# Storing half of x and loading six experts' down weights in the convolution's time instead of in routing's

## The reference

```python
x = x + attention(layernorm(x))                       # 16 heads, ALiBi
x = x + xattn(ctx, ctx, layernorm(x), ssm_kernel, D)  # long convolution
x = x + ffn(layernorm(x))                             # 8 experts, top 2

# ffn
probs = softmax(hs @ router_gate.T)
topk_scores, topk_idx = top_k(probs, 2)               # scores are then divided by their sum
inter = x_e @ expert_gate_up[e];  gate, up = inter[..., 0::2], inter[..., 1::2]
out_rows = (up * silu(gate)) @ expert_down[e]
out.at[token_slots].add(out_rows * scores)
```

## Time and profile before

| | |
|---|---|
| runs | 1652.3, 1651.71, 1643.85 us; median 1651.71 us |
| profiled execution | 1653.92 us, its span 1652.2 us |
| PE busy | 1477.3 us, 89% of the span |
| DVE, ACT, POOL busy | 1046.5, 764.9, 664.3 us |
| DMA | 172.22 MB, mean 104 GB/s |

### The profile page before, as it was taken

One profiled execution on the slowest core, in us unless ns is written; L12 is line 12 of the kernel. 1 busy time (PEld: TensorE's weight loads), 2 busy tenths in 40 slices (PEclk: granted clock), 3 DMA queues, 4 the chain that ended last, 5 costly groups with the idle time before them and its releaser, 6 DMA issues. The chain is left out here.

```text
span 1652.2 us, 33234 instructions
## 1 busy us (share of the span) xinstructions
PE 1477.3 (89%) x8665; PEld 1192.3 (72%) x8666; DVE 1046.5 (63%) x3146; ACT 764.9 (46%) x2010; POOL 664.3 (40%) x842
## 2 busy tenths in 40 slices
PE   5899999999999999869998799978643999999997
PEld 5788888888888888747776677757642666666665
DVE  4777777777777777756888888886653323333332
ACT  3777777777767677733322323202321332222232
POOL 2011111111111111036886388843665555555553
PEclk9999999999999999979999999985555999999999
DMA  5544434343444343634124011115993555555552
GB/s 160 128 110 107 102 80 102 87 101 90 102 102 102 89 101 90 213 127 145 52 55 155 13 52 57 52 32 179 243 228 80 98 99 99 95 97 98 101 101 44
DMA packets 89776, 172.22 MB, mean 104 GB/s; under 512 B 26384, under 2 KB 26384, under 8 KB 88656
## 3 DMA queue, kind: packets, MB, share of 16 engines
q1 hardware_dynamic: 63584, 122.46, 27.8%
q0 software_dynamic: 18176, 35.80, 12.1%
q10 hardware_dynamic: 7920, 12.93, 3.2%
HBM read 78.10 MB, written 44.79 MB: 74 GB/s over the span
## 5 line engine op out<-in xcount | busy, mean ns | idle before, releaser
L1135 PE MATMUL ps_y<-pairs,taps 128*128 128x288 f32 x1280 | 311.1, 406 | 5.4 <-ACT q_g L1201 3.2
L1135 PEld LDWEIGHTS ps_y<-pairs,taps 128*128 128x128 f32 x1280 | 242.9, 190 | 73.2 <-issue 6.2
L853 ACT ACTIVATE probs<-neg_scores,neg_max 128x256 f32<-128x256 f32 x512 | 255.3, 505 | 25.6 <-DVE neg_max L654 25.4
L654 DVE CUSTOM_DVE_ANT_0 neg_scores<-ps_scores,alibi 128x256 f32<-128x256 f32 x512 | 194.9, 418 | 89.8 <-PE ps_scores L519 60.9
L863 ACT ACTIVATE probs_t<-ps_probs_t 128x512 f32<-128x512 f32 x208 | 124.0, 596 | 131.3 <-PE ps_probs_t L530 131.3
L1606 POOL DMA_INDIRECT out<-y_row,back x72 | 113.2, 1572 | 175.4 <-DMA out<-y_row,back 140.6
L530 PE MATMUL ps_probs_t<-ident,probs 128*128 128x128 f32 x1024 | 158.8, 279 | 9.7 <-ACT probs L853 9.7
L403 POOL COPY inv_wide<-inv_sum 128x512 f32<-128x512 f32 x32 | 20.6, 673 | 317.3 <-DVE inv_sum L670 317.3
L1993 DVE TENSOR_TENSOR st_lo<-ps_x,st_hi 128x512 fp32r<-128x512 f32 x72 | 49.8, 691 | 145.9 <-ACT st_hi L1784 145.8
L530 PEld LDWEIGHTS ps_probs_t<-ident,probs 128*128 128x128 f32 x1024 | 123.9, 143 | 23.5 <-ACT probs L853 10.1
L1166 ACT ACTIVATE q_ring<-q_g 128x512 f32 (+1 forms) x64 | 40.1, 630 | 213.7 <-DVE ps_y L1246 213.6
(11 more groups left out here) (198 smaller groups left out, 3578.7 us busy)
## 6 DMA issues: line engine op xcount, KB each, us to landing
q_stack<-q_hi SPq DMA_DIRECT2D x128, 128.0 KB, 2.3
k_stack<-k_hi SPq DMA_DIRECT2D x128, 128.0 KB, 2.3
taps<-kernel_pad SPq DMA_DIRECT2D x64, 256.0 KB, 3.1
x_in<-in_x SPq DMA_DIRECT2D x16, 512.0 KB, 3.6
q_stack<-q_lo SPq DMA_DIRECT2D x64, 128.0 KB, 2.3
k_stack<-k_lo SPq DMA_DIRECT2D x64, 128.0 KB, 2.3
x_rows<-x_mid SPq DMA_DIRECT2D x16, 512.0 KB, 3.0
ctx_g<-in_ctx_t SPq DMA_DIRECT2D x2, 4096.0 KB, 12.2
```

The costliest lines, as they stand in the source:

```text
L654: last = dve.tensor_tensor_reduce(neg_scores[h % 2][:, tt, :], ps_scores[h % 2][:, tt, :], alibi[h % 2][:, P - P * tt:P - P * tt + T], -Q_ ...
L853: last = act.activation(probs[h % 2][:, tt, :], neg_scores[h % 2][:, tt, :], ACT.Exp, bias=neg_max[par][:, h, tt:tt + 1], scale=-1.0, accu ...
L1135: last = pe.matmul(ps_y[par][:, lc, :].rearrange("p (b q) -> p b q", b=GB)[:, :, 0:PAIRS], taps[r][:, block_cols:block_cols + P], pairs[r] ...
```

## The change

Two kinds of transfers move from routing into the convolution, both to ACT's queue. In group 0, behind its first `turn_q`, ACT issues six experts' down weights (512 KB each). In group 1, at the same place, it issues one store of all 16 tiles of the first group's x (4 MB). Routing keeps the down weights of the last two experts, which SP now issues ahead of the router weights, and the store of the second group's x, in four parts for e = 0 to 3, each behind that expert's two `w_half` loads instead of ahead of them.

To make room for `w_down` in the convolution, tiles change places in SBUF, and `xn_g` becomes a view of `prods`. The loop over batches is written out in full on every engine.

```diff
@@ layout
-            w_down = sbuf("w_down", [P, NE, FC, E], scope=last_of_all)
...
         with ExitStack() as later:
             ctx_g = sbuf("ctx_g", [P, EC, GB * T], scope=later)
             x_res = sbuf("x_res", [P, NT, E], scope=later)
+            w_down = sbuf("w_down", [P, NE, FC, E], scope=later)
@@ convolution
-            xn_g = [sb(f"xn_g{i}", [P, TT, E]) for i in range(2)]
+            xn_g = [to[:, 0:EC * GB // 2, :, :].rearrange("p n d i -> p (n d i)").rearrange("p (t e) -> p t e", e=E)
+                    for to in prods]
...
                     turn_q(g, 0, 0)
+                    if g == 0:
+                        for e in range(NE - 2):
+                            act.dma_start(w_down[:, e, :, :], down[e].rearrange("(c p) n -> p c n", p=P))\
+                               .then_inc(w_down_load, 16)
+                    else:
+                        act.wait_ge(x2_ready, GT + X2_START)
+                        act.dma_start(out_tiles[:, 0:GT, :], x_res[:, 0:GT, :]).then_inc(x2_stored, 16)
                     quads(act, lambda k, r: head_step(g, k, r))
@@ routing
-            X2_STORES = NE
+            X2_STORES = 1 + NE // 2
+            X2_TILES = GT // (NE // 2)
...
             def route_steps(eng, emit):
-                rounds(eng, ROUNDS, 2, lambda k, par, last: emit(k, par, last and par == 1))
+                for k in range(ROUNDS):
+                    for par in range(2):
+                        emit(k, par, k == ROUNDS - 1 and par == 1)
+            def stored_by(e):
+                return 16 if e < NE // 2 else (e - NE // 2) * 16 + 32
...
             def _(sp):
+                for e in (NE - 2, NE - 1):
+                    sp.dma_start(w_down[:, e, :, :], down[e].rearrange("(c p) n -> p c n", p=P)).then_inc(w_down_load, 16)
                 sp.dma_start(w_router[:], router_t.rearrange("(c p) n -> p c n", p=P)).then_inc(router_load, 16)
                 for e in range(NE):
-                    sp.wait_ge(n_ready, e * (NT // NE) + 1)
-                    if e:
-                        sp.wait_ge(x2_stored, e * 16)
-                    tiles = slice(e * (NT // X2_STORES), (e + 1) * (NT // X2_STORES))
-                    sp.dma_start(out_tiles[:, tiles, :], x_res[:, tiles, :]).then_inc(x2_stored, 16)
-                    sp.dma_start(w_down[:, e, :, :], down[e].rearrange("(c p) n -> p c n", p=P)).then_inc(w_load, 16)
+                    sp.wait_ge(n_ready, e * BATCH + 1)
                     for half in range(2):
...
+                    if e < NE // 2:
+                        sp.wait_ge(x2_stored, e * 16 + 16)
+                        tiles = slice(GT + e * X2_TILES, GT + (e + 1) * X2_TILES)
+                        sp.dma_start(out_tiles[:, tiles, :], x_res[:, tiles, :]).then_inc(x2_stored, 16)
...
                 def split_hi(e):
-                    act.wait_ge(x2_stored, e * 16 + 16)
+                    act.wait_ge(x2_stored, stored_by(e))
```

More of the change, by code:

```diff
@@ L95, in build_decoder @@
         with ExitStack() as last_of_all:
-            w_down = sbuf("w_down", [P, NE, FC, E], scope=last_of_all)
+            with ExitStack() as routing:
+                xn_c = [sbuf(f"xn_c{i}", [P, E], scope=routing) for i in range(8)]
+                w_half = [sbuf(f"w_half{i}", [P, 2, 2 * FI], scope=routing) for i in range(2)]
+            srow = [sbuf(f"srow{i}", [P, E], scope=last_of_all) for i in range(6)]
+            y_row = [sbuf(f"y_row{i}", [P, E], scope=last_of_all) for i in range(4)]
+            st = [[sbuf(f"st_{part}{i}", [P, EC, P], F32R, scope=last_of_all) for part in ("hi", "lo")] for i in range(2)]
+            sbuf("ctx_g_rest", [P, T, EC], scope=last_of_all)
             w_gu_hi = sbuf("w_gu_hi", [P, NE, EC, 2 * FI], F32R, scope=last_of_all)
@@ L973, in build_decoder @@
             sbuf("x_res_place", [P, NT, E])
+            sbuf("w_down_place", [P, NE - 2, FC, E])
+            ctx_ring = [sb(f"ctx_ring{i}", [P, EC * GB, 2 * SD]) for i in range(2)]
+            q_ring = [sb(f"q_ring{i}", [P, EC * GB, 2 * SD]) for i in range(2)]
             q_g = sb("q_g", [P, EC, GB * T])
@@ L977, in build_decoder @@
             prods = [sb(f"prods{i}", [P, EC * GB, SD, SD]) for i in range(2)]
-            q_ring = [sb(f"q_ring{i}", [P, EC * GB, 2 * SD]) for i in range(2)]
-            ctx_ring = [sb(f"ctx_ring{i}", [P, EC * GB, 2 * SD]) for i in range(2)]
-            xn_g = [sb(f"xn_g{i}", [P, TT, E]) for i in range(2)]
+            xn_g = [to[:, 0:EC * GB // 2, :, :].rearrange("p n d i -> p (n d i)").rearrange("p (t e) -> p t e", e=E)
+                    for to in prods]
             ps_y = [psum(f"ps_y{i}", [P, EC, E], scope) for i in range(2)]
@@ L1003, in build_decoder @@
             x2_rstd = sem("x2_rstd")
+            x2_stored = sem("x2_stored")
+            w_down_load = sem("w_down_load")
             Y_START, PRODS_START, XT_START, X2_START = TAP_BUFS, 2, 2, 8
@@ L1298, in build_decoder @@
         assert NE == 8 and N_TILES % RING == 0 and N_BATCHES % 2 == 0 and ROUNDS >= 2 and RING % BUFS == RING % ROW_BUFS == 0
+        sbuf("w_down_last_place", [P, 2, FC, E])
         with ExitStack() as scope:
@@ L1315, in build_decoder @@
             with ExitStack() as routing:
-                xn_c = [sb_in(routing, f"xn_c{i}", [P, E]) for i in range(2 * BATCH)]
-                w_half = [sb_in(routing, f"w_half{i}", [P, 2, 2 * FI]) for i in range(2)]
                 xt_c = [sb_in(routing, f"xt_c{i}", [P, EC, P]) for i in range(2)]
@@ L1362, in build_decoder @@
                 back = [sb_in(tiling, f"back{i}", [P, 1], U32) for i in range(RING)]
-                srow = [sb_in(tiling, f"srow{i}", [P, E]) for i in range(ROW_BUFS)]
-                st = [[sb_in(tiling, f"st_{part}{i}", [P, EC, P], F32R) for part in ("hi", "lo")] for i in range(2)]
                 silu_g = [sb_in(tiling, f"silu_g{i}", [P, FI]) for i in range(2)]
@@ L1368, in build_decoder @@
                 hidden_t = [sb_in(tiling, f"hidden_t{i}", [P, FC, P]) for i in range(2)]
-                y_row = [sb_in(tiling, f"y_row{i}", [P, E]) for i in range(BUFS)]
             ps_x = psum("ps_x", [P, 2, E], scope)
@@ L1379, in build_decoder @@
             router_load = sem("router_load")
-            w_load = sem("w_load")
             w_half_load = [sem(f"w_half_load{i}") for i in range(2)]
@@ L1420, in build_decoder @@
             y_scattered = [sem(f"y_scattered{i}") for i in range(BUFS)]
-            x2_stored = sem("x2_stored")
             NT_START, ST_LO_START, HIDDEN_START, DOWN_START, Y_START, KEPT_START = 2, 2, 2, 2, 2, 1
@@ L1730, in tile_step @@
                     down_rows(kk, r, e)
-                pe.wait_ge(w_load, 16 * NE)
+                pe.wait_ge(w_down_load, 16 * NE)
                 for half in range(2):
```

## The result

The changed kernel takes 1644.8 us (median of 19 runs, 1641.9 to 1649.3), the one before 1649.7 us beside it (19 runs, 1642.3 to 1653.4). The ratio is 0.9976, 95% interval 0.9966 to 0.9987: 4.9 us less, where 12.2 us were forecast. The profiled execution took 1646.87 us with a span of 1645.2 us.

What follows compares the result with a forecast made beforehand. Routing, paced by POOL's and DVE's beats with waits on transfers, delays the PE-bound tiles. Saving 13.4 - 1.2 = 12.2 us takes the profiled 1653.9 to 1641.7, the median to 1639.5; predicted 1640 us, range 1636 to 1646.

Steps and rivals of the forecast that it cites:

- the price of the moved transfers in routing: Routing: moving 7 MB out shortens the beat, 13.4 us saved less 1.2 us of waits left, 12.2 us.
- the base: Routing: six steps from batch 1's to batch 7's scatters take 90.6 us, 15.1 us each, read from one execution.
- the waits left: Routing, experts 1 to 3: x stores still mix with row stores, 0.4 us each, 1.2 us; bounds 0 and 10.0.
- ACT's issues: Convolution, group 0: six issues on ACT take 3.1 us, at most 10.4, within 9.2 us of slack; cost 0.
- the stores stay slow: Rival, routing: mixing queues keeps row stores slow; only 4 to 8 us saved, 1644 to 1648 us; chance 0.20.
- the text's own rule: Routing: the slower loop, DVE's at 12.86 us, rules; saving is 6 x (15.10 - 12.86) = 13.4 us.
- The signs that the text named for itself: Routing, changed trace: POOL's wait for ACT's rounded part below 3 us, DVE's for stores below 2 us, if right.
- ACT is held by its queue: Rival, convolution: issues behind 4 MB of x hold ACT 19 or 32 us; 1662 us at 32; chance 0.08.
- The slack: Convolution: ACT's second `q_ring` ends at 748.90 and DVE takes it at 758.14, so 9.2 us of delay is free.
- Router weights later: Routing's start: router weights up to 5.3 us late, covered by PE's 8.2 us stand after batch 1; cost 0.
- Loops at 0: Routing: loops over batches written out, bounds -2.0 and +1 us, taken as 0.
- Taps: Convolution: taps land near 6 us beside added traffic but are issued some 14 us before use; cost 0.

Runs made afterwards that it cites:

- no_x_in_routing: Changed kernel with six down loads issued in group 0's last four heads and the second group's four x stores left out (output incomplete); ratio 0.9953 to the kernel before.
- x_early: Changed kernel with six down loads in group 0's last four heads and second group's x stored in one transfer at routing's start; 1635.4 us, ratio 0.9926.

## Why the prediction was wrong

The step that failed is the price of the moved transfers in routing, 13.4 - 1.2 = 12.2 us. With the same places in SBUF the steps went from 83.8 us (the mean of four executions) to 82.6 in the changed kernel, 1.2 us, and to 80.1 and 81.0 with the issues in a better place. Both terms of the sum were mis-sized, the base and the waits left, and two more things put at 0 or left out, ACT's issues and the change of places, were not 0. The time of 1644.8 us lies within 1636 to 1646 by luck: the kernel before was at 1649.7 us in the longer comparison and not at 1651.7, and the 4 us that the tiles gave stood in no step. It lies within 1644 to 1648 of the rival "the stores stay slow" too, but the mechanism of that one did not happen: the row stores landed in 5.7 us instead of 8.9.

*The sum's base.* The sum started from "six steps in 90.6 us, 15.1 us each". It was read rightly from one execution, the slowest of three; the mean is 88.2, so 14.7 us each. With the text's own rule that leaves 6 x (14.7 - 12.86) = 11.0 us to win, not 13.4. Some 4 us of these (88.2 - 83.8) came with the places and not with the transfers.

*The waits left.* I took 0.4 us for each of three steps, 1.2 us in all, near the lower end of 0 to 10. The steps came to 82.6 us where 78.4 were forecast: 4.2 us more, most of it one wait of 4.39 us of POOL. The signs that the text named for itself say the same: POOL's wait was to fall below 3 us and was 5.1, DVE's below 2 and was 5.6. That transfers delay the row stores and DVE passes this on was right, as no_x_in_routing and x_early show, and so was the floor: without an x store in the loop the steps take 78.0 us, near 6 x 12.86 = 77.2. The size was wrong: 82.6 - 77.2 = 5.4 us of waits were left, not 1.2. The x stores behind `w_half` still met the row stores.

*ACT's issues.* "I take 0, since nothing but the issue is asked of ACT here." They took 11.6 and 12.7 us, beyond my upper bound of 10.4, and made PE stand 1.69 and 2.62 us; in all group 0 was 2.2 and 4.5 us longer. The rival "ACT is held by its queue" had the mechanism: the issues stand behind 4 MB. It priced it too high (19 to 32 us), since ACT is free again well before the data have landed: the median landing is 13.3 us after the issue, the last issue ended at 760.8 us and ACT went on at 760.82. What spoke for it, SP's 1.74 us, I set aside as "far from 3 us each"; it may have been the same effect with less ahead. The slack was nearly as worked out, 9.2 us: ACT came 11.0 us late, PE stood 1.69 us.

*The change of places.* The text priced the diff's transfers, loops and queues and gave the moved tiles no term. They are worth 4 us in the tiles' stage, where the text said that PE is busy all the time: exactly for that reason each nanosecond on a matmul counts there. 72 tiles x 12 matmuls x 4 ns (the mean of 3, 5 and 4) is 3.5 us, which is most of it.

*Right.* Router weights later: PE's stand behind batch 1 fell from 8.25 to 4.23 us, and the first scatter kept its distance to group 1's first transpose back, 41.8 us (1146.11 - 1104.35). Loops at 0: 0.9998. Taps: 6.2 us to landing beside the new load, and no wait of PE for them. The store in group 1: 0.4 us for its issue and nothing lost to it. `w_half` landed in 6.1 us.

The parts of the 4.9 us are, against the mean of the three executions before: steps -5.6, tiles -4.0 (386.8 to 382.8), group 0 +3.4, group 1 +3.0 by the clock. That is -3.2 us from two executions of the changed kernel, beside -4.9 us from the medians of 19 runs each. The spans themselves differ by 0.9 us only, mainly because these two came 2.7 us later to the first convolution matmul (at 749.5 us on average instead of 746.8). Both kernels spread by 7 to 11 us, so the two profiled executions may have been slower than most; that was not measured. Of the gain, no part that can be measured comes from the transfers as they were moved: the places alone give 0.9967 or 0.9961, the whole change 0.9976, with intervals that overlap. With the issues in a better place the whole gives 0.9948, and with the rest of x out of the loop 0.9926.

## What to carry to other kernels

Put bulk transfers where no engine waits for anything, and never behind megabytes in the queue of an engine that has other work: the same six loads cost nothing from an empty queue. A change that moves tiles in SBUF has a term for it in the sum, above all in a stage that one engine fills; test the layout apart from the rest. Before a sum rests on one execution, see whether the stretch that it uses repeats: it was 86.7, 87.3 and 90.6 us here.

## What the runs showed of the hardware

- The place of a stationary operand in SBUF changes the matmuls' cadence: 397 and 394 ns with st at byte 196704 or 217184, 392 and 390 ns at 38912 or 116736. The cause was not found. The first two are 32 past a multiple of 64 and the other two multiples of 1024, so alignment fits as well as height; between byte 124928 and 196704 nothing was tried.
- An issue takes 0.37 to 0.58 us from an empty queue and up to 3.88 us behind 4 MB in the same queue (ACT, six of 512 KB: 11.6 us), and it holds the engine's own instructions behind it. Another engine's issues at that time took 0.33 us each.
- Around or after a stand of PE of 2 to 3 us the granted clock can be lower (0.79 over 8 us, 0.91 over 20 us), in some executions and not in others, and once it was at 0.76 over 7 us without a stand of that length.
